# The mixture-of-experts stage of a four-layer transformer as straight-line rounds of four sequences, and key parts written to DRAM one step later

## The reference

```python
x = x + _L0_xattn_ref(_layernorm(x), ctx, Wq, Wk, Wv, Wo, bo)   # 8 heads of 64
x = x + _L0_ffn_ref(_layernorm(x), gate_w, wg, wu, wd, sg, su, sd)
x = x + _L1_xattn_ref(_layernorm(x), ctx, ctx, ...)             # 16 heads of 8
x = x + _L1_ffn_ref(...)                                        # nvfp4
x = x + _L2_xattn_ref(...); x = x + _L2_ffn_ref(...)            # fp8
x = x + _L3_xattn_ref(...); x = x + _L3_ffn_ref(...)            # bitlinear
```

```python
scores = softmax(xf @ gate_w.T)                 # 8 experts
_, idx = top_k(scores, 2)
cw = zeros((N, 8)).at[arange(N)[:, None], idx].add(take_along_axis(scores, idx))
h = silu(einsum('nd,efd->nef', xf, wg)) * einsum('nd,efd->nef', xf, wu)
routed = einsum('ned,ne->nd', einsum('nef,edf->ned', h, wd), cw)
shared = silu(xf @ sg.T) * (xf @ su.T) @ sd.T
return routed + shared
```

## Time and profile before

| | |
|---|---|
| median of 3 runs | 829.3 us (825.61 to 832.38) |
| the profiled execution | 826.71 us, of which the recorded span is 824.3 us |
| PE busy | 543.9 us (66%) |
| DVE busy | 524.3 us (64%) |
| ACT busy | 414.7 us (50%) |
| POOL busy | 297.6 us (36%) |
| granted TensorE clock, mean | 0.791 of full speed |

### The profile page before, as it was taken

The page is one execution under the profiler, slowest core; times in us unless marked ns, Lnnn a source line. Parts: engine busy times, 40 slices in busy tenths (PEclk is TensorE's granted clock), DMA queues, the critical chain, the costliest instruction groups (busy, mean ns, idle before and its releaser), DMA issues.

```text
span 824.3 us, 19004 instructions
## 1 busy us (share of the span) xinstructions
PE 543.9 (66%) x5619; PEld 357.2 (43%) x5619; DVE 524.3 (64%) x1608; ACT 414.7 (50%) x1037; POOL 297.6 (36%) x559
## 2 busy tenths in 40 slices
PE   5788889847888678887322432799996138793352
PEld 4576667634544454554101211455564026561131
DVE  2767676645777557776788885466775853326673
ACT  2666667733222236665435764565563014445674
POOL 2444444424555423342024326344430023323510
PEclk9999999978999759999555555599999557876555
DMA  8832333310000033432000001233330015550001
GB/s 228 212 69 62 67 64 64 69 31 0 1 0 0 18 79 91 113 96 59 10 1 0 0 0 40 53 88 89 91 91 17 0 39 142 133 137 2 0 0 52
DMA packets 102629, 47.51 MB, mean 58 GB/s; under 512 B 82160, under 2 KB 92080, under 8 KB 102448
## 3 DMA queue, kind: packets, MB, share of 16 engines
q1 hardware_dynamic: 102576, 46.87, 22.6%
HBM read 26.92 MB, written 19.92 MB: 57 GB/s over the span
## 4 chain that ended last, share of the span: by engine, by line
issue 29%; PE 20%; DVE 17%; POOL 12%; ACT 5%; DVEq 5%; DMA 5%; POOLq 3%; SPq 2%; ACTq 0%
PE bank L510 3%; DMA scratch_q<-q_parts 3%; PE bank L444 3%; POOL small L1362 2%; PE bank L459 2%; PE bank L551 2%; DMA stacks<-scratch_q 2%; POOL tmp_a L1250 2%; DVE xn L1604 2%; POOL stats L1222 2%; PE bank L476 1%; DVE small L1445 1%; DVE mx L1628 1%; PE bank L590 1%; POOL tmp_b L1250 1%
## 5 line engine op out<-in xcount | busy, mean ns | idle before, releaser
L1628 DVE TENSOR_REDUCE mx<-bank 128x4 f32<-128x512 f32 x160 | 103.8, 683 | 22.0 <-PE bank L459 20.3
L909 ACT ACTIVATE probs<-bank 128x512 f32<-128x512 f32 x160 | 90.9, 595 | 48.3 <-PE bank L480 46.2
L1283 POOL CAST q_parts<-resid 128x128 bf16<-128x128 f32 x48 | 14.2, 296 | 94.8 <-DVE resid L1643 94.8
L1643 DVE SCALAR_TENSOR_TENSOR resid<-bank,w_bias_cols,q_parts 128x128 f32<-128x128 f32 x48 | 16.8, 350 | 49.2 <-ACT q_parts L959 49.2
L510 PE MATMUL bank<-probs,v_slot 128*9 128x128 f32 x1024 | 45.9, 299 | 3.0 <-ACT probs L909 0.8
L1222 POOL TENSOR_TENSOR stats<-stats,half_neg 128x1 f32<-128x1 f32 x48 | 26.2, 546 | 57.3 <-DVE stats L1599 57.1
L1109 ACT ACTIVATE att_t<-bank 128x512 f32<-128x512 f32 x16 | 9.6, 597 | 63.8 <-PE bank L780 63.8
L476 PE MATMUL bank<-stacks 48*128 48x128 bf16 x512 | 39.6, 228 | 1.9 <-DVE shift_t L1664 1.1
L480 PE MATMUL bank<-shift_t,pick_bf 64*128 64x128 bf16 x512 | 39.4, 227 | 0.3 <-issue 0.3
L546 PE MATMUL bank<-w_ident,xn 128*128 128x128 f32 x64 | 21.4, 334 | 27.0 <-DVE xn L1604 15.8
L982 ACT ACTIVATE att<-bank 128x512 f32<-128x512 f32 (+1 forms) x48 | 25.1, 522 | 23.3 <-PE bank L510 21.5
(11 more groups left out here) (298 smaller groups left out, 1756.6 us busy)
## 6 DMA issues: line engine op xcount, KB each, us to landing
stacks<-scratch_k SPq DMA_DIRECT2D x64, 96.0 KB, 2.2
stacks<-scratch_q SPq DMA_DIRECT2D x64, 96.0 KB, 2.2
scratch_k<-k_parts SPq DMA_DIRECT2D x48, 96.0 KB, 1.9
scratch_q<-q_parts SPq DMA_DIRECT2D x48, 96.0 KB, 1.9
scratch_k<-k_parts SPq DMA_DIRECT2D x48, 64.0 KB, 1.7
scratch_q<-q_parts SPq DMA_DIRECT2D x48, 64.0 KB, 1.7
stacks<-scratch_k SPq DMA_DIRECT2D x16, 192.0 KB, 2.6
stacks<-scratch_q SPq DMA_DIRECT2D x16, 192.0 KB, 2.5
```

What stands on the lines that cost most here:

```text
L909: activation(probs[:, slot, :], bank[2 + u % 2][:, :], ACT.Tanh if layer == 3 else ACT.Exp, scale=float(d) ** -0.5).then_inc(sm["p"], 1)
L1628: reduce(mx[:, sM, at * UNIT:(at + 1) * UNIT], bank[u % 2][:, :].rearrange("p (h k) -> p h k", h=UNIT), AX.X, ALU.max).then_inc(sm["mx"], 1)
```

## The change

Four things change.

1. SP writes the key parts of sequence t-2 in step t, where it wrote those of t-1.
2. FFN 0 becomes five straight-line rounds of four sequences. Round r computes logits, gate, up, the shared expert and the routing of group r, and turns the hidden values of group r-1 and computes its outputs. Layer norm (statistics on DVE, `deviations0` on POOL, `normalize0` on ACT instead of DVE), subtraction, power, sums and weights are done for four sequences in one instruction each; the largest two are still found per sequence. The shared expert comes out turned: weights times 512 tokens, two matmuls of 64x512 (`shared`), a silu of 64x512 on ACT and a product of 64x512 on DVE (`hidden_shared`), so the hidden values of the shared expert need no transpose (L780) and no copies.
3. The head of FFN 0's first group is written into attention 0's drain: statistics, deviations and `normalize0(0)` after the first drain step, transposes and copy after the second. Before, it was the first two sequences' normalization, and the second sequence's steps ran ahead to its gate and up. `turn_weights` now stands ahead of all of FFN 0's matmuls except the transposes.
4. Attention 1's two early steps stand inside FFN 0's last round: on PE between `turn_hidden` and `down`, on DVE ahead of `outputs(3)`, on POOL after the last `hh`. Layer 0 no longer counts a semaphore that nothing waits for.

The old step functions are in the listing above; of them the diff shows nothing.

```diff
                 if on(k, 0) and k >= SLOTS:
                     wait(sp, L0x["v_ps"], t - SLOTS + 1)
                     context(t, k)
-                if on(k, 1):
-                    s = (k - 1) % SLOTS
-                    wait(sp, L0x["kk_parts"], t)
+                if on(k, 2):
+                    s = (k - 2) % SLOTS
+                    wait(sp, L0x["kk_parts"], t - 1)
...
-            pipeline(sp, contexts, 1)
+            pipeline(sp, contexts, 2)
...
+            def turn_inputs0(g):
...
+                pe.wait_ge(f["xn"], (g + 1) * GROUP)
...
+                wait(pe, f["sgs"], g)
+                for j in range(GROUP):
+                    last = tr(bank[0][:, j * T:(j + 1) * T], xn[:, j, :], ident[:, :])
+                last.then_inc(f["yT_ps"], 1)
...
+                def shared(g):
+                    y = xn_t[:, :, :].rearrange("p s k -> p (s k)")
+                    mm(bank[0][0:F0, :], gs_w[:, E0:E0 + F0], y, start=True, stop=True).then_inc(f["gs_ps"], 1)
+                    pe.wait_ge(f["e"], g + 1)
+                    mm(bank[1][0:F0, :], gs_w[:, E0 + F0:E0 + 2 * F0], y, start=True, stop=True).then_inc(f["gs_ps"], 1)
...
+                for r in range(B // GROUP + 1):
+                    if r < B // GROUP:
+                        logits(r)
+                    for j in range(GROUP):
+                        if r:
+                            turn_hidden(r - 1, j)
+                        if r < B // GROUP:
...
+                            gate_up(r, j)
+                            if j == 1:
+                                shared(r)
+                            if j == 3 and r + 1 < B // GROUP:
+                                turn_inputs0(r + 1)
+                        elif j < EARLY:
+                            early(j, j, 0)
+                        if r:
+                            down(r - 1, j)
...
-            pipeline(pe, attention_step(0), 3, early=ffn0_step(), after=1)
+            pipeline(pe, attention_step(0), 3, early=ffn0_head)
             turn_weights()
-            pipeline(pe, ffn0_step(), 4, first=EARLY, early=attention_step(1))
+            ffn0(attention_step(1))
...
+            def normalize0(g):
...
+                act.wait_ge(ln_rstd, B + (g + 1) * GROUP)
...
+                for j in range(GROUP):
+                    activation(xn[:, j, :], x_sb[:, g * GROUP + j, :], ACT.Identity, scale=st[:, j, 9:10],
+                               bias=st[:, j, 10:11]).then_inc(F[0]["xn"], 1)
...
+                for r in range(B // GROUP + 1):
+                    for j in range(GROUP):
+                        if r:
+                            hidden_turned(r - 1, j)
+                        if r < B // GROUP:
+                            silu(r, j)
+                            if j == 1:
+                                silu_shared(r)
+                            if j == 2 and r + 1 < B // GROUP:
+                                normalize0(r + 1)
+                        elif j < EARLY:
+                            early(j, j, 0)
+                    if r + 1 < B // GROUP:
+                        inputs_turned0(r + 1)
...
+                for r in range(B // GROUP):
+                    pool.wait_ge(f["e"], r + 1)
+                    tt(route[r % 2][1], euler[:, :].rearrange("p (o e) -> p o e", o=1).to_broadcast([P, GROUP, E0]),
+                       route[r % 2][0], ALU.pow).then_inc(f["pw"], 1)
+                    for j in range(GROUP):
+                        if j == 1 and r + 1 < B // GROUP:
+                            deviations0(r + 1)
+                        if j == 0:
+                            pool.wait_ge(f["wt"], r + 1)
+                        pool.wait_ge(f["h"], r * GROUP + j + 1)
...
+                        tt(experts, experts, weight.to_broadcast([P, E0, F0]), ALU.mult).then_inc(f["hh"], 1)
+                for t in range(EARLY):
+                    early(t, t, 0)
...
+                def weights(g):
...
+                    copy(index, top[:, :, :])
+                    drain()
+                    tt(first, names, index[:, :, 0:1].to_broadcast([P, GROUP, E0]), ALU.is_equal)
+                    tt(both, names, index[:, :, 1:2].to_broadcast([P, GROUP, E0]), ALU.is_equal)
+                    drain()
+                    tt(both, both, first, ALU.add)
+                    drain()
+                    tt(weight, both, probs2, ALU.mult).then_inc(f["wt"], 1)
...
+                for r in range(B // GROUP):
+                    less(r)
+                    hidden(r, 0)
+                    if r + 1 < B // GROUP:
+                        stats4(r + 1, f, 1)
+                    hidden(r, 1)
+                    hidden_shared(r)
+                    probabilities(r)
+                    hidden(r, 2)
+                    drain()
+                    weights(r)
+                    hidden(r, 3)
+                    if r:
+                        outputs(r - 1)
+                for t in range(EARLY):
+                    early(t, t, 0)
+                outputs(B // GROUP - 1)
```

More of the change, by code:

```diff
@@ L171, in build_kernel @@
         q0, k0 = hid, gated
[L172 removed]
+        hs_t = sb("hs_t", [F0, 2, 4, T])
         tmp_a = sb("tmp_a", [P, 4 * P])
@@ L177, in build_kernel @@
         top = sb("top", [P, SLOTS, 8], U32)
-        from_x = resid[:, :, :, :].rearrange("p s l k -> p s (l k)")[:, :, 0:E0 + 2 * F0]
+        route_ = small[:, :, :, :].rearrange("p s i n -> p (s i n)")
+        route = [[route_[:, 384 * a + 4 * E0 * i:384 * a + 4 * E0 * (i + 1)].rearrange("p (j e) -> p j e", e=E0)
+                  for i in range(9)] for a in range(2)]
         work3 = sb("work3", [P, 4, F1])
@@ new lines, in each, with less @@
+                def each(ap):
+                    return ap.rearrange("p (j o) -> p j o", o=1).to_broadcast([P, GROUP, E0])
+                def less(g):
+                    psum = bank[1][:, 0:GROUP * E0].rearrange("p (j e) -> p j e", e=E0)
+                    low = route[g % 2][8].rearrange("p j e -> p (j e)")[:, 0:GROUP]
+                    dve.wait_ge(f["s_ps"], g + 1)
+                    reduce(low, psum, AX.X, ALU.max)
+                    drain()
+                    tt(route[g % 2][0], psum, each(low), ALU.subtract).then_inc(f["e"], 1)
@@ new lines, in hidden_shared, with outputs @@
+                def hidden_shared(g):
+                    dve.wait_ge(f["sgs"], g + 1)
+                    dve.wait_ge(f["gs_ps"], 2 * g + 2)
+                    wait(dve, f["o_ps"], (g - 1) * GROUP)
+                    tt(hs_t[:, g % 2, :, :].rearrange("p j k -> p (j k)"), tmp_a[0:F0, :], bank[1][0:F0, :], ALU.mult
+                       ).then_inc(f["hs"], 1)
+                def outputs(g):
+                    dve.wait_ge(f["o_ps"], (g + 1) * GROUP)
+                    x = flat(x_sb[:, seqs(g), :])
+                    tt(x, bank[7][:, :], x, ALU.add).then_inc(x_done, GROUP)
```

276 lines of the change are left out of this document (130 added, 146 removed).

## The result

The changed kernel takes 826.35 us (median of 8 runs, 823.67 to 827.29). Over the same eight runs the kernel before took 832.0 (825.61 to 838.76): the ratio is 0.9939, 95% interval 0.9917 to 0.9961. So it is faster by some 5 us of 832, less than half of the 12 forecast, and 826.35 lies outside the range of 805 to 825.

What follows compares the result with a forecast made beforehand. Context-load waits bounded attention 0, a dependent chain FFN 0. Attention 0's 9.9 us gain plus FFN 0 ending 1.4 earlier gave 815.4 from the profiled 826.7, 818.0 from the median; forecast 817 us, range 805 to 825.

Steps and rivals of the forecast that it cites:

- Part 1: Attention 0's eleven steps: earlier context loads remove the K products' waits, gaining 9.9 us, bounds 0 to 10.4.
- Part 2: Attention 0's drain: FFN 0's head and weight transposes placed there start FFN 0 5.3 us later, bounds 3 to 7.
- Part 3: FFN 0's four-sequence rounds up to attention 1's first scores: 101.1 us with clock falls, 89.3 at the full clock.
- The rival that part 1 doesn't do what it says: Attention 0: the load doesn't come earlier or another bound stands right behind it; total 827 us, chance 0.08.
- Both named causes: Drain: ACT's normalizations ahead of the last exponentials delay first logits by 1.2 us; `turn_weights` with its handoff adds 4.1.
- I let the clock fall once in each round: half of 3.3 us and the first work behind it, 2 us: FFN 0's rounds: each idle time of PE lowers the clock once, adding 2 us per round.
- 3.41 us was enough at 280.74: Late in the old FFN 0: PE's 3.41 us idle time taken as evidence that such waits lower the clock.
- The end was put at 39: Round 3 up to attention 1's first scores: 39 us at the lower clock, about 33.2 at the full one.
- The terms of DVE in the round, 4.9: DVE's part of a round's closing path: `hidden_shared` 0.7, probabilities 2.3, third product 0.7, weights 1.2 us.
- The lower clock lasts twice as long in each round: Rival for FFN 0's rounds: two us more in three rounds, 107 for 101; total 824 us, chance 0.16.
- The clock holds: Rival for FFN 0: full clock throughout, the stage ends 13.2 us earlier than before; total 806 us, chance 0.17.
- TensorE never gets back to the full clock: Rival for FFN 0: rounds stay at the lower clock, 33.6 us each; total 851 us, chance 0.05.

Runs made afterwards that it cites:

- second profile: The kernel before, unchanged, run and profiled again: ratio 0.9991, median 831.94 us, profiled span 828.5 us.
- the kernel with work in place of the wait: Kernel after plus three thrown-away 512-column matmuls on TensorE ahead of the next input transposes in each of the first three rounds: 818.68 us, ratio 0.9823.
- the kernel with FFN 0 alone: Kernel before with only FFN 0 rewritten and its head in the drain, key parts written as before: 835.14 us, ratio 1.0034.
- the first normalizations later: Kernel after with the first group's four ACT normalizations moved from the first to the second drain step, behind the last exponentials: 822.43 us, ratio 0.9860.
- the transposes in round 0: Kernel after with FFN 1's weight transposes moved from ahead of FFN 0 into its round 0: 818.27 us, ratio 0.9832.
- the kernel with the added work: Kernel after with deviations early, normalizations late, weight transposes in round 0, plus three thrown-away matmuls ahead of attention 1's first early step: 794.79 us, ratio 0.9581.
- the three moves alone: Kernel after with deviations ahead of the first expert multiplication, first normalizations later and weight transposes in round 0: 797.59 us, ratio 0.9595.

## Why the prediction was wrong

What waits for what in a round was forecast rightly. Its sizes were not: the price of the clock's fall above all, and a wait inside DVE's chain that was left out. Against the profiled execution of before the forecast was 815.4, and the profiled execution of after took 826.46: of these 11.1 us, parts 1 and 2 are 0.5 each, and part 3 is 10.1.

- **Part 1, key parts a step later.** Forecast 9.9; the profiled executions show 108.25 − 98.83 = 9.4, every step at the 8.9 to 9.0 of the step without a wait. Alone it was worth 12.2 in the medians and 112.04 − 100.36 = 11.7 in the profiles. The bound "10.4 as the most that the waits hold" was nearly right for the waits, 10.7 in the second profile; it left out that the clock can be low behind one, which took another 1.5 us there. The rival that part 1 doesn't do what it says fell.
- **Part 2, the drain.** Forecast 5.3 later, measured 42.42 − 36.65 = 5.8, with first logits at 183.83 where 183 was said. Both named causes were confirmed by moving them away: 2.7 us for the normalizations, 4.6 for the weight transposes, 42.42 to 35.1 with both. That the sum came out is in part luck: 1.2 and 4.1 were forecast for the two, 2.7 and 4.6 are together more than the drain grew by, and without either it is 1.5 us shorter than before (35.1 for 36.65), which was not in the sum.
- **Part 3, the rounds: the step that failed.** Forecast 101.1, measured 111.24. The step is "I let the clock fall once in each round: half of 3.3 us and the first work behind it, 2 us". It fell once a round as said, in rounds 2 and 3 behind a wait of 2.62 us where 2.7 were forecast; but the work behind it ran at the lower level for some 6.8 us (227.75 to 234.6; in round 1 from 203.85 to 210.7, where a `down` takes 1.16 again), and a round at the full clock is 20.62, so that the fall cost 3.3. I priced it by the one low stretch of before, 3.30 us, which was half as long. A round of 24.06 is thus 19.5 as forecast at the full clock, 0.3 more of PE's work (8.7 us to the end of `shared` at the full clock, 229.69 to 238.38 in the kernel with work in place of the wait, for 8.4), 0.8 more in DVE's chain (below) and 3.4 for the clock. Over rounds 1 and 2 and the end, the clock is some 5.9 of the 10.1 us, DVE's chain 2.4 and PE's work 0.9; round 0, 20.02 for 19.1, is the last 0.9.
- The reason given for the fall did not hold either. "3.41 us was enough at 280.74" takes the whole wait for its cause, and the window from 279.00 shows 0.50 already 1.7 us before that wait ended. Across these kernels the length of a wait alone did not decide it (last section).
- The end was put at 39 from a first part of 13.3 at the full clock: the fall of round 3 was left out of it. Measured, 11.9 us to the end of `shared` for 8.4. That is 3.5 of the 4.2 by which the end is longer, and DVE's chain behind it is 0.8; behind the first `hh` it took 25.65 where 25.7 was forecast.
- The terms of DVE in the round, 4.9, were 5.69. Their operations were priced 0.4 too high (4.5 without the wait), but `hidden(r, 2)` stands between the probabilities and the weights and waits 1.19 us for ACT's silu of the third gate. That wait on another engine in the middle of a chain was not in the sum; the weights put first took it out and showed it. (The prediction's own terms add up to 19.6, not 19.5.)
- Right were the power of 128x32, 5.43 us where the line through two sizes gave 5.4; POOL's 2.55; ACT's end of the round; and PE's own work, 17.8 at the full clock for 16.8, somewhat low (a `down` takes 1.4).
- **The rivals.** "The lower clock lasts twice as long in each round", 824 at 0.16, is nearest to what happened: low stretches of 6.8 us for 3.3, 107 us for FFN 0, and DVE's missed wait and the rest of round 3's fall on top. "The clock holds" came about in only one of eight rounds behind a wait of 2.62 or 2.63 us, in the kernel with FFN 0 alone. That TensorE never gets back to the full clock was not seen: PEclk was 0.85 and 0.86 in rounds 1 and 2. The rule of the Trainium skill (TensorE: Matmul & The Clock Gate, section "HAM oscillation — how this bites in real kernels"), pieces that start cold behind a recurring wait, held in rounds 1 to 3 of the kernel after, behind waits of 5.02, 2.62 and 2.63 us; in the kernel with FFN 0 alone one of two rounds kept its clock behind the same 2.62 us.
- Of the forecast signs, logits 19 to 22 us apart came true once in three: they were 20.0, 24.1 and 23.9 apart.
- Where the gain went: the key parts bring about 12 us, the drain gives back 5.8, and FFN 0 gives back 3.8 (111.24 for 107.40 in the second profile of before). That leaves 2.4 where the medians differ by 5.6; the rest is not located, and profiles of one kernel differ by as much. The fall of the clock, at 3.3 us in each of three rounds, is more than the 3.8: with it out, as an estimate from these two numbers, the stage would have been some 101 us, shorter than before. The kernel with work in place of the wait had it at 101.99 (186.99 to 288.98).

## What to carry to other kernels

When work is grouped, the path that closes a group must be looked for by name: here the next group's layer norm stood behind this group's routing on one engine's list, and one line moved was worth 21.5 us, nearly four times the change itself. A wait of TensorE that recurs in each round is to be priced with its own length and with what runs at the lower clock behind it; work thrown into the wait can be cheaper than the wait. And one profiled execution is one draw: its waits were in sum those of the next, but not the steps at the lower clock, so compare its time with the median before a bound is taken from it.

## What the runs showed of the hardware that was not expected

In the kernel before, PE ahead of the low stretch of the earlier trace rows:

```profile
213.54 0.48 PE L789 MATMUL bank<-w_sd,hs_t 64*128 64x128 f32 x2 [1.12 <-DVE hs_t L1892]
213.96 1.99 PE L791 MATMUL bank<-w_wd,att_t 128*128 128x128 f32 x8
```

The wait just ahead of it was 1.12 us, shorter than the 2.02 us of the earlier trace rows behind which the K products ran at the full clock.

- A wait of the same length does not always do the same to the clock. Four kernels (after, FFN 0 alone, the first normalizations later, the transposes in round 0) had two rounds each that begin behind a wait of 2.62 or 2.63 us: in seven of these eight the logits took 1.71 or 1.72 us, at the lower level, and in one 0.96. Behind 0.73 and 1.09 they took 0.96 both times. In these seven the clock fell not in the wait but 1.2 to 1.9 us after its end, with TensorE at work.
- Attention 0 shows the same. In the second profile of before, the K products behind waits for the context of 2.77 and 2.97 us took 1.15 us, and those behind 1.91 us took 2.01, in a step 1.5 us longer. Removing the waits took 11.7 us off the eleven steps, for waits of 10.7.
- The clock kept through FFN 0's end fell in the stage behind it: in the kernel with the added work it went to the lower level at 264.5, in the three moves alone at 270.5. That may be why 3.9 us of the profiles' end are 2.8 in the medians; no run here isolates it.
